# Row maxima turned by VectorE in place of TensorE, and squares set around the statistics of the mix

## The reference

```python
attn = einsum('bhqd,bhkd->bhqk', query, key) / scale      # 16 heads of 32
attn = softmax(attn, axis=-1)
x = x + (einsum('bhqk,bhkd->bhqd', attn, value)) @ Wo_w + Wo_b
xn = layernorm(x)
x_prev = concatenate([zeros, xn[:, :-1]], axis=1)
xr = mu_r * xn + (1.0 - mu_r) * x_prev
xk = mu_k * xn + (1.0 - mu_k) * x_prev
r = sigmoid(xr @ W_r.T)
k_act = square(relu(xk @ W_k.T))
out = x + r * (k_act @ W_v.T)
```

## Time and profile before

| | us |
|---|---|
| median of 3 runs (lowest, highest) | 3019.98 (3019.28, 3020.96) |
| the profiled execution | 3021.54 |
| its span, first to last instruction | 3019.8 |
| TensorE matmul busy | 2965.3 (98%) |
| VectorE busy | 2198.5 (73%) |
| GpSimd busy | 2012.0 (67%) |
| ScalarE busy | 1481.9 (49%) |

### The profile page before, as it was taken

One profiled execution on the slowest core, in us unless ns is written; L12 is line 12 of the kernel. 1 busy time (PEld: TensorE's weight loads), 2 busy tenths in 40 slices (PEclk: granted clock), 3 DMA queues, 4 the chain that ended last, 5 costly groups with the idle time before them and its releaser, 6 DMA issues. The chain is left out here.

```text
span 3019.8 us, 42725 instructions
## 1 busy us (share of the span) xinstructions
PE 2965.3 (98%) x15424; PEld 2002.6 (66%) x15424; DVE 2198.5 (73%) x3371; ACT 1481.9 (49%) x2716; POOL 2012.0 (67%) x704
## 2 busy tenths in 40 slices
PE   8999999999999999999999999999999999999999
PEld 5888888865555555555555555555547777787777
DVE  5555566597777877777777777777787777677774
ACT  2222222236666666666666666666663323323232
POOL 1111111229999999999999999999953555565553
PEclk9999999999999999999999999999999999999999
DMA  4455555764646464646464646464551332323321
GB/s 151 168 176 175 171 171 178 209 165 103 151 103 151 103 151 102 151 102 151 102 151 102 151 102 151 102 151 103 136 151 48 107 96 71 111 60 107 96 70 42
DMA packets 189081, 380.72 MB, mean 126 GB/s; under 512 B 17376, under 2 KB 53376, under 8 KB 180992
## 3 DMA queue, kind: packets, MB, share of 16 engines
q1 hardware_dynamic: 180000, 313.70, 37.7%
q0 software_dynamic: 8928, 65.02, 10.5%
HBM read 194.59 MB, written 118.49 MB: 104 GB/s over the span
## 5 line engine op out<-in xcount | busy, mean ns | idle before, releaser
L444 DVE TENSOR_REDUCE part_max<-ps_m 128x1 f32<-128x512 f32 x1984 | 1210.9, 684 | 279.4 <-PE ps_m L428 278.7
L1156 POOL TENSOR_TENSOR pairs<-probs 128x2048 f32<-128x2048 f32 x248 | 1153.3, 4661 | 111.1 <-ACT probs L1130 110.9
L1130 ACT ACTIVATE probs<-ps_s 128x512 f32<-128x512 f32 x2012 | 1016.6, 623 | 262.1 <-PE ps_s L1021 245.8
L428 PE MATMUL ps_m<-k_stack,q_stack 96*128 96x512 f32 x1984 | 818.4, 413 | 2.1 <-PEq L476 2.1
L1021 PE MATMUL ps_s<-q_stack,k_stack 97*128 97x512 f32 x2012 | 795.5, 397 | 0.0
L428 PEld LDWEIGHTS ps_m<-k_stack,q_stack 96*128 96x128 f32 x1984 | 376.9, 190 | 238.6 <-DVE part_max L444 104.5
L1034 PE MATMUL ps_o<-probs,v_tiles 128*32 128x512 f32 x4096 | 492.5, 598 | 0.0
L1021 PEld LDWEIGHTS ps_s<-q_stack,k_stack 97*128 97x128 f32 x2012 | 380.7, 189 | 105.6 <-ACT probs L1130 2.8
L1163 POOL TENSOR_TENSOR pairs<-pairs 128x2048 f32<-128x2048 f32 x62 | 284.3, 4585 | 4.9
L691 POOL TENSOR_TENSOR ln_rstd<-ln_rstd,ln_minus_half 128x4 f32<-128x4 f32 x15 | 15.1, 1009 | 403.9 <-DVE ln_rstd L733 403.9
L1034 PEld LDWEIGHTS ps_o<-probs,v_tiles 128*32 128x32 f32 x4096 | 107.0, 109 | 234.3 <-issue 174.9
(11 more groups left out here) (200 smaller groups left out, 4900.6 us busy)
## 6 DMA issues: line engine op xcount, KB each, us to landing
pairs<-pairs POOLq DMA_DIRECT2D x62, 1024.0 KB, 8.0
q_stack<-q_hi_scratch SPq DMA_DIRECT2D x128, 256.0 KB, 5.5
k_stack<-k_hi_scratch SPq DMA_DIRECT2D x64, 512.0 KB, 10.9
x_in<-in_x SPq DMA_DIRECT2D x16, 1024.0 KB, 5.6
q_hi_scratch<-st_hi SPq DMA_DIRECT2D x64, 256.0 KB, 2.3
q_lo_scratch<-st_lo SPq DMA_DIRECT2D x64, 256.0 KB, 2.6
k_hi_scratch<-st_hi SPq DMA_DIRECT2D x64, 256.0 KB, 2.4
k_lo_scratch<-st_lo SPq DMA_DIRECT2D x64, 256.0 KB, 2.7
```

The lines of the kernel that those rows point to most:

```text
L428: nc.tensor.matmul(bank[:, :], att["q"][r][0:ROWS, half, h, q * P:(q + 1) * P], att["k"][r][0:ROWS, h, kc * CH:(kc + 1) * CH], start=True, ...
L444: nc.vector.reduce_max(part_max[:, half, j, kc:kc + 1], bank[:, :], AX).then_inc(att["m_read"], 1)
L1130: nc.scalar.activation(probs[:, (r * UNITS + u) % PR, x // HG, x % HG, :], bank(n, place(u * UT + x))[:, :], ACT.Exp, scale=SCALE).then_in ...
L1156: nc.gpsimd.tensor_tensor(pairs[:, w, :, :], probs[:, (r * UNITS + u) % PR, 0, :, :], probs[:, (r * UNITS + u) % PR, 1, :, :], ALU.add).th ...
```

## The change

It has two parts that don't touch each other.

The row maxima are no longer transposed by TensorE. `row_max` is one tile of 128 x 32 with a half in each 16 columns, set to 0 once. When VectorE has reduced a half, it waits for that result and transposes the tile in four blocks of 32 x 32, one for each 32 partitions (`turned_max`). SP writes a half's maxima to row 96 of q with four transfers of 16 pieces of 128 bytes, where it was one of 16 pieces of 512 bytes. Row 96 of k holds -1 in place of 1, so no step has to change the sign. `USE`, `SPREAD`, `AFTER` and the banks follow: 64 steps, all tiles.

In the mix GpSimd's inverse root moves from ahead of the four squares to between the second and the third. VectorE's low part of the first square moves ahead of the last two row statistics (behind xr_lo), that of the second between the statistics and the normalising.

```diff
-            nc.vector.memset(att["k"][0][ROWS:ROWS + 1, :, :].bitcast(F32), 1.0)
+            nc.vector.memset(att["row_max"][:, :].bitcast(F32), 0.0)
+            nc.vector.memset(att["k"][0][ROWS:ROWS + 1, :, :].bitcast(F32), -1.0)
...
-USE = (tiles(0, 0, HALF_TILES) + tiles(1, 0, UNIT_TILES) + [(0, HALF_TILES, 0)]
-       + tiles(1, UNIT_TILES, HALF_TILES) + [(1, HALF_TILES, 0)])
+USE = tiles(0, 0, HALF_TILES) + tiles(1, 0, HALF_TILES)
...
-    bank = banks[BANK[u]]
-    if EARLIER[u] >= 0 or not is_first(m):
-        pe.wait_ge(att["m_read"], m * USES + EARLIER[u] + 1)
-    if j == HALF_TILES:
-        pe.wait_ge(att["m_rows"], m * 2 + half + 1)
-        nc.tensor.transpose(bank[0:HALF_TILES, 0:P], att["row_max"][:, half, :], ident[:]).then_inc(att["m_scored"], 1)
-        return
+    bank = banks[u % MR]
+    if u >= MR or not is_first(m):
+        pe.wait_ge(att["m_read"], m * USES + u - MR + 1)
...
-    if j == HALF_TILES:
-        if half == 1 or not is_first(m):
-            dve.wait_ge(att["m_stacked"][1 - half], 16 * (m + half))
-        nc.vector.tensor_scalar(neg_max[:, :], bank[0:HALF_TILES, 0:P], -1.0, None,
-                                ALU.mult).then_inc(att["m_read"], 1)
-        return
...
-        nc.vector.reduce_max(row_max[:, half, :], part_max[:, half, :, :], AX).then_inc(att["m_rows"], 1)
+        nc.vector.reduce_max(row_max[:, half * HALF_TILES:(half + 1) * HALF_TILES], part_max[:, half, :, :], AX).then_inc(att["row_done"], 1)
+        if not is_first(m):
+            dve.wait_ge(att["m_stacked"][half], 16 * BLOCKS * m)
+        dve.wait_ge(att["row_done"], m * 2 + half + 1)
+        nc.vector.transpose(att["turned_max"][:, half, :].bitcast(F32), row_max[:, :].bitcast(F32)).then_inc(att["m_rows"], 1)
...
-    sp.wait_ge(att["m_read"], n * USES + ROWS_AT[half] + 1)
+    sp.wait_ge(att["m_rows"], n * 2 + half + 1)
     sp.sem_inc(held, 1)
-    sp.dma_start(att["q"][r][ROWS:ROWS + 1, half, :, :].bitcast(F32).rearrange("o a t -> o (a t)"),
-                 att["neg_max"][:, :].bitcast(F32)).then_inc(att["m_stacked"][half], 16)
+    row = att["q"][r][ROWS:ROWS + 1, half, :, :].bitcast(F32).rearrange("o a (q p) -> o (a q) p", p=P)
+    for i in range(BLOCKS):
+        first = i * BLOCK + half * HALF_TILES
+        sp.dma_start(row[:, :, i * BLOCK:(i + 1) * BLOCK],
+                     att["turned_max"][first:first + HALF_TILES, half, :].bitcast(F32)).then_inc(att["m_stacked"][half], 16)
...
-    AFTER = [2] * 7 + [3] * 5
+    AFTER = [2] * 8 + [3] * 4
...
-        SPREAD[ROUNDS][UT] = 1
-        SPREAD[UNITS - 1][UT] = 1
...
-                    if more:
-                        inv_std(c + 1)
                     for g in range(FC):
+                        if g == RELU and more:
+                            inv_std(c + 1)
                         pool.wait_ge(relu_done, c * FC + g + 1)
...
                 shift_low_r(c - 1)
+                square_lo(0)
                 for s in range(0 if type(c) is int and c == 1 else TPC - 2, TPC):
                     row_stats(c, par, s)
                 statistics(c)
+                square_lo(1)
                 normalise(c, par)
...
-                    for g in range(FC):
+                    for g in range(2 if more else 0, FC):
                         square_lo(g)
```

More of the change, by code:

```diff
@@ L291, in tiles @@
     return [(half, j, kc) for j in range(first, last) for kc in range(KCS)]
-UNIT_TILES = HALF_TILES // 4
-USE = (tiles(0, 0, HALF_TILES) + tiles(1, 0, UNIT_TILES) + [(0, HALF_TILES, 0)]
-       + tiles(1, UNIT_TILES, HALF_TILES) + [(1, HALF_TILES, 0)])
+USE = tiles(0, 0, HALF_TILES) + tiles(1, 0, HALF_TILES)
 USES = len(USE)
 STEPS = USES
-ROWS_AT = [USE.index((half, HALF_TILES, 0)) for half in range(2)]
-BANK = [(sum(j < HALF_TILES for _, j, _ in USE[:u]) + (USE[u][1] == HALF_TILES)) % MR for u in range(USES)]
-EARLIER = [max(v for v in range(-USES, u) if BANK[v] == BANK[u]) for u in range(USES)]
+BLOCK = 32
+BLOCKS = P // BLOCK
 LOADS = 3 * NQ + 3
@@ L411, in load_group, with max_product @@
     sp.dma_start(att["v"][r][:], v_d[n]).then_inc(att["v_loaded"][r], 16)
-def max_product(nc, pe, att, banks, ident, m, r, loads, u):
+def max_product(nc, pe, att, banks, m, r, loads, u):
     half, j, kc = USE[u]
-    bank = banks[BANK[u]]
-    if EARLIER[u] >= 0 or not is_first(m):
-        pe.wait_ge(att["m_read"], m * USES + EARLIER[u] + 1)
-    if j == HALF_TILES:
-        pe.wait_ge(att["m_rows"], m * 2 + half + 1)
-        nc.tensor.transpose(bank[0:HALF_TILES, 0:P], att["row_max"][:, half, :], ident[:]).then_inc(att["m_scored"], 1)
-        return
+    bank = banks[u % MR]
+    if u >= MR or not is_first(m):
+        pe.wait_ge(att["m_read"], m * USES + u - MR + 1)
     if u == 0:
@@ L434, in max_reduce @@
     half, j, kc = USE[u]
-    bank = banks[BANK[u]]
-    part_max, row_max, neg_max = att["part_max"], att["row_max"], att["neg_max"]
+    part_max, row_max = att["part_max"], att["row_max"]
     dve.wait_ge(att["m_scored"], m * USES + u + 1)
-    if j == HALF_TILES:
-        if half == 1 or not is_first(m):
-            dve.wait_ge(att["m_stacked"][1 - half], 16 * (m + half))
-        nc.vector.tensor_scalar(neg_max[:, :], bank[0:HALF_TILES, 0:P], -1.0, None,
-                                ALU.mult).then_inc(att["m_read"], 1)
-        return
-    nc.vector.reduce_max(part_max[:, half, j, kc:kc + 1], bank[:, :], AX).then_inc(att["m_read"], 1)
+    nc.vector.reduce_max(part_max[:, half, j, kc:kc + 1], banks[u % MR][:, :], AX).then_inc(att["m_read"], 1)
     if j == HALF_TILES - 1 and kc == KCS - 1:
         dve.wait_ge(att["m_read"], m * USES + u + 1)
-        nc.vector.reduce_max(row_max[:, half, :], part_max[:, half, :, :], AX).then_inc(att["m_rows"], 1)
+        nc.vector.reduce_max(row_max[:, half * HALF_TILES:(half + 1) * HALF_TILES], part_max[:, half, :, :], AX).then_inc(att["row_done"], 1)
[3 more added lines that the diff above has]
+        nc.vector.transpose(att["turned_max"][:, half, :].bitcast(F32), row_max[:, :].bitcast(F32)).then_inc(att["m_rows"], 1)
 def stack_max(sp, held, att, n, r, half):
-    sp.wait_ge(att["m_read"], n * USES + ROWS_AT[half] + 1)
+    sp.wait_ge(att["m_rows"], n * 2 + half + 1)
     sp.sem_inc(held, 1)
-    sp.dma_start(att["q"][r][ROWS:ROWS + 1, half, :, :].bitcast(F32).rearrange("o a t -> o (a t)"),
-                 att["neg_max"][:, :].bitcast(F32)).then_inc(att["m_stacked"][half], 16)
+    row = att["q"][r][ROWS:ROWS + 1, half, :, :].bitcast(F32).rearrange("o a (q p) -> o (a q) p", p=P)
[3 more added lines that the diff above has]
+                     att["turned_max"][first:first + HALF_TILES, half, :].bitcast(F32)).then_inc(att["m_stacked"][half], 16)
 def project_block(nc, sem, held, t, w, x_v, x_in, x_loaded, ln, att, grouped, scratch):
@@ L621, in body @@
                     final = last and par == CPB - 1
-                    todo = list(range(STEPS - 1)) if final else []
+                    todo = list(range(STEPS)) if final else []
                     def maxima(count):
                         for _ in range(count if todo else 0):
-                            max_product(nc, pe, att, ps_m, t["ident"], 0, 0, 1, todo.pop(0))
+                            max_product(nc, pe, att, ps_m, 0, 0, 1, todo.pop(0))
                     rotated(c, par)
@@ L1611, in normalise, with norm @@
                 v.then_inc(normed, 1)
[L1613 removed]
+            def norm(c, par, square_lo):
                 for s in range(TPC):
@@ L1782, in block_program @@
             "part_max": lasting("part_max", [P, 2, HG * QT, KCS]),
-            "row_max": lasting("row_max", [P, 2, HG * QT]),
-            "neg_max": lasting("neg_max", [HG * QT, P], F32R),
+            "row_max": lasting("row_max", [P, 2 * HG * QT], F32R),
+            "turned_max": lasting("turned_max", [P, 2, BLOCK], F32R),
+            "row_done": sem("row_done"),
             "loaded": [sem(f"stack_loaded{r}") for r in range(R3)],
```

11 lines of the change are left out of this document (4 added, 7 removed).

## The result

| us | before | after |
|---|---|---|
| median (lowest, highest) | 3019.99 (3019.28, 3020.96), 4 runs | 2983.02 (2981.69, 2983.85), 4 runs |
| the profiled execution, its span | 3021.54, 3019.8 | 2981.69, 2979.9 |
| TensorE matmul busy | 2965.3 (98%) | 2944.0 (99%) |

The ratio is 0.9877, with a 95% interval of 0.986 to 0.9894: 37.0 us less, where the prediction said 32.0 and its range ended at 36 (2984). The direction and the places were right, the size of the largest term was not.

What follows compares the result with a forecast made beforehand. TensorE was taken to pace both attention and the mix. The terms -9.9 + 1.9 + 0.1 - 24.1 = -32.0 took the profiled 3021.54 to 2989.5, 2988 us as median; forecast 2984 to 2991, whole range 2984 to 2998.

Steps and rivals of the forecast that it cites:

- Transposes out of TensorE, -9.9: Attention: 62 transposes at 0.16 us each leave TensorE, 9.9 us less, if VectorE's new step makes TensorE wait for nothing.
- the room of 1.06 us: Attention: time VectorE has from row_max's start before TensorE must wait; the new step was put at 0.58 us.
- Four transfers, +1.9: End of the projection: three more SP issues (1.6 us) and VectorE's transpose (0.3) delay attention's start by 1.9 us.
- the transpose ahead of the last v tile (+0.3): End of the projection: VectorE's transpose stands ahead of the last v tile that SP waits for, 0.3 us more.
- the memset (+0.1): Start: setting row_max's 32 columns once costs 0.1 us, at most 0.19.
- The mix, -24.1: Mix, r product: TensorE's 15 waits for the third relu go, 21.7 us plus 15 x 0.16, 24.1 us less.
- that stretch keeps its length: Mix, from the transposes to the k product: the same work hangs on VectorE and starts no later, so no change.
- (a): Rival, mix: xr_lo comes late and TensorE stops 0.1 to 0.4 us in 14 chunks, up to 5.6 us: 2994; chance 0.12.
- Normalising: Mix, VectorE: normalising takes 3.3 us and ends by 2681.9, leaving 3 us before TensorE's transposes need it.
- (b): Rival: attention gives nothing, VectorE's step exceeds 1.06 us or GpSimd at 95% takes over: 2998; chance 0.10.
- (c): Rival, attention: VectorE's transpose waits for GpSimd's pair sum, 62 x 3.3 = 205 us, 3193; chance 0.06.
- (d): Rival: the mix's stop only moves, another input of r being as late: 3012; chance 0.06.

Runs made afterwards that it cites:

- the nine transposes: After, with nine more transposes of the same tile into a spare tile behind each one in attention: 2991.09 us (one run).
- Moving the issues: After, with SP issuing the four transfers of group 0's second half at the start of attention, not at the projection's end: 2980.97 us, on another chip 2979.84.
- root alone: Before, with only GpSimd's inverse root moved behind the second square, all four low parts of VectorE staying behind the normalising: 3007.93 us.
- the copy: After, with a plain 128 x 32 copy from SBUF to SBUF into a spare tile behind each transpose on VectorE: 3335.66 us (one run).
- the mix alone: Before, with only the mix's edits (root behind second square, low parts 0 and 1 moved earlier), maxima still turned by TensorE: 2990.74 us.

## Why the prediction was off, point by point

- **What bounds the kernel**: right. Both stages followed TensorE.
- **Transposes out of TensorE, -9.9**: right within the spread (-10.8; 1585.5 to 1587.8 between executions). The estimate of 0.24 us was 0.21, the wait for its own result about 0.11 (1000.30 + 0.19 to 1000.60) where 0.15 was taken, and the room of 1.06 us was right to 0.1 us by the nine transposes. The units that began with a transpose fell by 0.17 us on average, 5.97 to 5.80 and 7.68 to 7.51, which is 10.3 in all. Units with sums that never had a transpose took 7.53 before and 7.50 to 7.53 in the executions after it, so the rest is not tied to a cause.
- **Four transfers, +1.9**: right, about +2.0. Two kernels with before's code up to there and the same granted clock as after from 20 to 40 us (0.91) started attention at 651.29 and 651.38, after at 653.17. The four issues took 2.42 us where one took 0.52, 1.9 more and not 1.6. What the transpose ahead of the last v tile (+0.3) and the memset (+0.1) cost, no run shows. Moving the issues took 2.3 us back.
- **The mix, -24.1**: the step that failed, mis-sized: it measured -28.5. The mechanism was right (no relu among the waits, third relu in time). The term counted the stop only to the start of the next matmul, and left out the slow restart (1.7 us). And the sentence "that stretch keeps its length" was wrong: the earlier low parts let the division begin earlier, diff is held less, the gates are in time, and o and v lost some 2.3 us of small delays. The prediction itself noted, in its rival (a), that the division leaves diff alone, and gave that no value.
- **Normalising**: taken as 3.3 us of work, where 1.4 were being held (and the two squares beside it as 2.22, where they take 2.04 alone). It did no harm to the sum, since in after the third and fourth squares lie beside it and it takes 3.36 again, but it made the expectation for the root alone wrong by 21 us.
- **The rivals**: (a) did not come, xr_lo ended at 2646.19, 1.0 us ahead of r (2647.23); (b) no; (c) no, though the copy shows that its place and mechanism exist, and that its price would have been 353 us and not 205; (d) no.
- **The range**: its lower end allowed for no cost at the start and 2 us of spread, and for nothing that a removed stop gives back further on. A term of the 4.4 us that came on top would have put it near 2980.

Two executions of one kernel differ before attention begins. The stretch of 20 to 40 us (columns as above), before, then the mix alone, whose code is the same up to there:

```profile
20.00:40.00 20.00, 17.54 (x59) 10.07 (x59) 12.22 (x34) 3.49 (x10) 1.03 (x1) 0.83 0.16 51
```

```profile
20.00:40.00 20.00, 17.53 (x68) 9.60 (x67) 12.41 (x34) 3.85 (x11) 1.03 (x1) 0.91 0.16 51
```

The granted clock is 0.83 in one and 0.91 in the other: by these means it was at 0.50 for some 6.8 of the 20 us and for some 3.4. Attention starts at 652.86 and at 651.38. That is why the profiled pair showed only 0.3 us of the 1.9, and 39.9 us in all where the medians differ by 37.0.

## What to carry to other kernels

Price a stop by the whole stretch from before it to the next steady point, restart included, and follow what its end releases: here, waits of 0.1 us that recurred in each chunk were its echo. When two engines share work on SBUF, compare an instruction's time in a place where the other engine is idle before taking it for its length; moving a step is also moving what it holds. And issue transfers behind the point where all engines meet, if their data are read later.

## What the runs showed of the hardware

- A 128x32 fp32 transpose on VectorE takes 0.211 us with GpSimd idle and 0.211 to 0.214 in the middle of its pair sums (62 times), and 0.093 from start to start in a row. A copy of the same size is held there: 0.137 us or 3.74.
- GpSimd is held too: its inverse root of 128x4 takes 1.02 us in before and 1.42 in after, where VectorE's low part started 0.15 us ahead of it. With the root moved and the low part not (root alone) it takes 1.02.
- A stop of 2.3 us in attention cost 5.7 us, since the granted clock was at the lower level for 6.8 us behind it. The stops of 1.4 us in the mix had no such price: the clock there is 1.00 in the earlier trace rows.
